# A tail of its own for the last full step, K norms from a triangle of the Gram matrix, and two attention answers moved

## What is computed

```python
xn = layernorm(x)
# attention, per batch, linear in the tokens
Q, K, V = xn @ Wq.T + bq, xn @ Wk.T + bk, xn @ Wv.T + bv
Q, K = Q / norm(Q, axis=tokens), K / norm(K, axis=tokens)
tailor = 1 / (256 + einsum('bnc,bc->bn', Q.T, K.sum(-1) + 1e-6))
s = xn + gamma * (V.sum(-1) + einsum('bnm,bmc->bcn', Q.T, einsum('bmn,bcn->bmc', K, V))) * tailor
# feed-forward, 704 hidden, activations and weights quantised to FP4 in blocks of 16
g = silu(fp4_linear(silu(fp4_linear(xn, w_gate)) * fp4_linear(xn, w_up), w_down))
out = x + s * g
```

## Time and profile before

| | |
|---|---|
| median of 3 runs | 596.38 us (595.67 to 596.96) |
| the profiled execution's own time | 597.39 us |
| its span in the trace | 595.3 us |
| busy: PE, DVE, ACT, POOL | 549.7, 555.4, 416.8, 265.6 us |
| mean granted TensorE clock | 0.991 |

### The profile page before, as it was taken

The page is one execution under the profiler, slowest core; times in us unless marked ns, Lnnn a source line. Parts: engine busy times, 40 slices in busy tenths (PEclk is TensorE's granted clock), DMA queues, the critical chain, the costliest instruction groups (busy, mean ns, idle before and its releaser), DMA issues. The chain is left out here.

```text
span 595.3 us, 15174 instructions
## 1 busy us (share of the span) xinstructions
PE 549.7 (92%) x4957; PEld 426.7 (72%) x4957; DVE 555.4 (93%) x1178; ACT 416.8 (70%) x901; POOL 265.6 (45%) x214
## 2 busy tenths in 40 slices
PE   0478999999999999999999989999999999999896
PEld 0355767777787777777887757778787777778775
DVE  7998999999999999999999998999999999977763
ACT  4979878877778777776777667877776776654421
POOL 7533333333433555355544453354743453423226
PEclk9999999999999999999999989999999999999999
DMA  8010000000011001111110111111011111132033
GB/s 251 18 37 19 19 20 19 19 20 19 19 37 37 19 3 55 55 55 55 55 55 2 54 58 55 56 55 54 2 55 55 55 37 37 36 103 95 0 124 143
DMA packets 17488, 29.14 MB, mean 49 GB/s; under 512 B 2688, under 2 KB 4864, under 8 KB 17408
## 3 DMA queue, kind: packets, MB, share of 16 engines
q1 hardware_dynamic: 17408, 28.13, 14.4%
HBM read 19.73 MB, written 8.39 MB: 47 GB/s over the span
## 5 line engine op out<-in xcount | busy, mean ns | idle before, releaser
L1427 PE MATMUL GU<-wgu,xqT 128*128 128x352 f16 x1536 | 252.8, 315 | 4.1 <-DVE h L953 2.6
L1427 PEld LDWEIGHTS GU<-wgu,xqT 128*128 128x128 f16 x1536 | 148.5, 99 | 78.3 <-issue 4.1
L546 POOL TENSOR_TENSOR ht<-h,hrr 128x1408 f32<-128x1408 f32 x32 | 82.9, 2590 | 80.5 <-DVE hrr L967 79.0
L635 ACT ACTIVATE sil<-GU,wkap 128x352 f32<-128x352 f32 x128 | 71.0, 555 | 60.0 <-PE GU L1427 59.1
L1437 PE MATMUL DS<-wdT,hqT 128*128 128x256 f16 x704 | 88.4, 275 | 1.9 <-ACT hqT L642 1.9
L953 DVE SCALAR_TENSOR_TENSOR h<-GU,wkap,sil 128x352 f32<-128x352 f32 x128 | 69.1, 540 | 11.9 <-ACT sil L635 8.0
L1001 DVE TENSOR_TENSOR hq<-hg,hs 128x704 f16<-128x704 f16 x128 | 79.1, 659 | 1.0
L1437 PEld LDWEIGHTS DS<-wdT,hqT 128*128 128x128 f16 x704 | 67.3, 99 | 12.5 <-ACT hqT L642 2.3
L505 POOL TENSOR_TENSOR xnat<-xs,xnat 128x510 f16<-128x510 f32 (+1 forms) x32 | 37.0, 1158 | 85.3 <-DVE hq L1001 72.9
L495 POOL TENSOR_TENSOR rs<-ve,half 128x2 f32<-128x2 f32 x32 | 22.9, 717 | 112.2 <-DVE ht L990 106.5
L671 ACT ACTIVATE gring<-DS,hun 128x256 f32<-128x256 f32 (+1 forms) x64 | 30.0, 468 | 44.9 <-issue 30.9
(11 more groups left out here) (166 smaller groups left out, 975.5 us busy)
## 6 DMA issues: line engine op xcount, KB each, us to landing
xin<-in_L_attn_x SPq DMA_DIRECT2D x34, 256.0 KB, 2.9
xe<-in_L_attn_x SPq DMA_DIRECT2D x25, 256.0 KB, 2.8
out<-o SPq DMA_DIRECT2D x25, 256.0 KB, 2.0
algebra<-in_L_ffn_w_down SPq DMA_DIRECT2D x1, 704.0 KB, 6.2
gring<-in_L_ffn_w_up SPq DMA_DIRECT2D x1, 640.0 KB, 4.8
xs<-in_L_attn_x SPq DMA_DIRECT2D x2, 256.0 KB, 4.2
xt<-in_L_attn_x SPq DMA_DIRECT2D x2, 256.0 KB, 4.7
out<-xin SPq DMA_DIRECT2D x2, 256.0 KB, 4.1
```

The source lines that it names most:

```text
L546: g.tensor_tensor(paired(ht[:, 0:2 * I]), paired(h[:, q]), spread(hrr[:, q], 4 * CB), ALU.mult).then_inc(S["ht_d"], 1)
L635: a.activation(sil[:, c], GU[:, c, 0, 0:CH], ACT.Silu, scale=wkap[:, 0:1]).then_inc(S["sil_d"], 1)
L1427: last = t.matmul(GU[:, c, m, 0:CH], xqT[:, k, j, 2 * a_ + kc], wgu[:, b_, kc, 2 * m + c], start=(z == 0 and kc == 0), stop=(z == 2 and kc ...
```

## The change

There are five edits. (1) K norms: G is symmetric, so t1k multiplies the diagonal blocks once and the lower block with a doubled copy of Wk, which ACT makes once (`wkT_twice`). (2) In the loop tables, gram1's answer moves in front of the mean and variance (`x_var`), and high_low's in front of the block maxima of x (`x_scales`, part 0). (3) p = 32 is taken out of `drive` for ACT, DVE and PE and written out by hand in their tails. (4) The last eight y's each get a place of their own, in h, ht, y and (for pair 31) the PSUM tile G; pair 24's x is loaded ahead too, into h, and POOL's add for pair 22 waits for the last scaled copy of pair 31. (5) The last pair's add is done by DVE, in halves, each stored by a DMA of its own.

```diff
-        ANSWERS = {(0, 0, 3): "gram0", (1, 0, 1): "gram1", ... (5, 0, 2): "high_low"}
+        ANSWERS = {(0, 0, 3): "gram0", (1, 0, 5): "gram1", ... (5, 0, 4): "high_low"}
@@ ACT, copy, at the start
+                    if i:
+                        a.activation(wkT_twice[:, :], G[:, D:2 * D], ACT.Copy, scale=2.0)
@@ PE, ask, t1k
                     for m in range(KD):
-                        for k in range(KD):
-                            last = t.matmul(G[:, m * D:(m + 1) * D], wkT[:, k, m * P:(m + 1) * P], Gs[:, k],
-                                            start=(k == 0), stop=(k == KD - 1))
+                        own = slice(m * P, (m + 1) * P)
+                        t.matmul(G[:, m * D:m * D + P], wkT[:, 0, own], Gs[:, 0, 0:P], start=True, stop=False)
+                        t.matmul(G[:, m * D:m * D + P], wkT_twice[:, own], Gs[:, 1, 0:P], start=False, stop=True)
+                        last = t.matmul(G[:, m * D + P:(m + 1) * D], wkT[:, 1, own], Gs[:, 1, P:D], start=True, stop=True)
@@ SP
+                        for j in range(2):
+                            own = slice(j * D, (j + 1) * D)
+                            sp.wait_ge(S["last_d"], j + 1)
+                            sp.dma_start(rows(of, e)[:, own], end_row(p)[:, own]).then_inc(S[f"out_d{ko}"], 16)
...
+                if isinstance(p, int) and p == PAIRS:
+                    sp.wait_ge(S["ht_d"], PAIRS - 1)
+                    sp.dma_start(h[:, 0, 0:2 * D], rows(xf, PAIRS - PB)).then_inc(S["x_mid_in"], 16)
@@ POOL, before the add
+                    if isinstance(e, int) and e == PAIRS - LAGE:
+                        pool.wait_ge(S["hloq"], 2 * PAIRS)
@@ DVE
+            def y_last(j):
+                return G[:, j * D:(j + 1) * D]
+            def o_last(j):
+                own = slice(j * D, (j + 1) * D)
+                dve.wait_ge(S["xend_in"], 16 * ENDS)
+                dve.wait_ge(S["y_d"], 4 * PAIRS - 2 + 2 * j)
+                v.tensor_tensor(xend[ENDS - 1][:, own], y_last(j), xend[ENDS - 1][:, own], ALU.add).then_inc(S["last_d"], 1)
...
             def tail():
+                p, k, b = PAIRS, PAIRS % 2, BATCHES - 1
+                e_half(p, k, 0, 0)
+                answer(b, "product")
+                parts(p, k, 0)
+                parts(p, k, 1)
+                e_half(p, k, 0, 1)
+                answer(b, "top")
+                answer(b, "high_low")
+                e_mul(p, k, 0)
+                e_mul(p, k, 1)
+                parts(p, k, 2)
+                h_round(p, k, 0)
+                e_mul(p + 1, 1 - k, 0)
+                h_round(p, k, 1)
+                e_mul(p + 1, 1 - k, 1)
+                h_round(p, k, 2)
+                e_mul(p + 2, k, 0)
+                e_mul(p + 2, k, 1)
+                h_round(p, k, 3)
+                for p in range(PAIRS + 3, PAIRS + LAGE):
                     for j in range(2):
                         e_mul(p, p % 2, j)
+                        if p == PAIRS + LAGE - 1:
+                            o_last(j)
@@ PE, tail
+                p, k = PAIRS, PAIRS % 2
+                s_half(p, k, 0, 0, last, PB - 5)
+                for c in range(2):
+                    hidden_transposes(p, k, 0, c, False)
+                ask(last, "product")
+                s_half(p, k, 0, 1, last, PB - 5)
+                down_product(p, k, 0)
+                ask(last, "top")
+                s_product(p, k, 0, last, False)
+                for c in range(2):
+                    hidden_transposes(p, k, 1, c, False)
+                ask(last, "high_low")
+                s_product(p, k, 1, last, False)
+                s_pair(PAIRS + 1 - LAGE)
+                down_product(p, k, 1)
-                p, k, first = PAIRS + 1, (PAIRS + 1) % 2, PAIRS + 1 - LAGE
+                p, k, first = PAIRS + 1, (PAIRS + 1) % 2, PAIRS + 2 - LAGE
                 s_pair(first)
                 s_pair(first + 1)
```

More of the change, by code:

```diff
@@ L213, in build @@
             nrm_d inv_d n_tr n_ev raw_mm raw_ev cs_mm cs_ev pm_mm den1 gi_d
[L214 removed]
+            tmp_d mt_d mtop_d last_d top_mm kap1 kap_d unm_d m_tr mhi_d mats""".split()
         S = {n: sem(n) for n in names}
@@ L264, in build @@
                 (5, 0, 1): "high_low"}
-        ANSWERS = {(0, 0, 3): "gram0", (1, 0, 1): "gram1", (1, 1, 0): "turn", (2, 1, 0): "squares",
-                   (3, 0, 0): "norms", (4, 0, 0): "tailor", (4, 0, 3): "scale", (4, 1, 0): "product", (4, 1, 2): "top", (5, 0, 2): "high_low"}
+        ANSWERS = {(0, 0, 3): "gram0", (1, 0, 5): "gram1", (1, 1, 0): "turn", (2, 1, 0): "squares",
+                   (3, 0, 0): "norms", (4, 0, 0): "tailor", (4, 0, 3): "scale", (4, 1, 0): "product", (4, 1, 2): "top", (5, 0, 4): "high_low"}
         COPIES = {(-4, 1, 0): "rows_1", (-3, 0, 1): "weights_v", (2, 0, 1): "t1q", (3, 1, 0): "raw"}
@@ L271, in build @@
                     (0, 1, 0): "gram1_0", (0, 1, 1): "gram1_1", (1, 0, 0): "turn", (1, 0, 2): "t1q",
-                    (1, 1, 1): "t1k", (2, 0, 0): "norms", (2, 0, 2): "raw", (2, 1, 1): "tailor", (3, 0, 0): "product",
-                    (3, 0, 1): "top", (3, 0, 3): "high_low"}
+                    (1, 1, 1): "t1k", (2, 0, 0): "norms", (2, 0, 2): "raw", (2, 1, 1): "tailor"}
         ANSWERS_END = {(0, 0, 2): "gram0", (0, 1, 2): "gram1", (1, 0, 1): "turn", (1, 1, 2): "squares",
-                       (2, 0, 1): "norms", (2, 1, 2): "tailor", (2, 1, 3): "scale", (3, 0, 0): "product",
-                       (3, 0, 1): "top", (3, 0, 4): "high_low"}
+                       (2, 0, 1): "norms", (2, 1, 2): "tailor", (2, 1, 3): "scale"}
         COPIES_END = {(1, 1, 0): "t1q", (2, 1, 0): "raw"}
@@ L303, in drive @@
                     iteration(b * PB + i, i % 2, b + later, step)
-            for p in range((BATCHES - 1) * PB + 4, PAIRS + 1):
+            for p in range((BATCHES - 1) * PB + 4, PAIRS if tail else PAIRS + 1):
                 iteration(p, p % 2, *batch_step(p))
@@ L324, in at_end, with y_place @@
         def at_end(p):
-            return isinstance(p, int) and p - LAGO >= PAIRS - ENDS
+            return isinstance(p, int) and p - LAGO >= PAIRS - PB
+        def y_place(e):
+            n = e - (PAIRS - PB) + 1
+            if n < 4:
+                return h[:, n // 2, n % 2 * 2 * D:(n % 2 + 1) * 2 * D]
+            return ht[:, (n - 4) * 2 * D:(n - 3) * 2 * D] if n < 7 else y[:, 0]
         def end_row(p):
-            return xend[p - LAGO - (PAIRS - ENDS)]
+            n = p - LAGO - (PAIRS - ENDS)
+            return h[:, 0, 0:2 * D] if n < 0 else xend[n]
         def s_beside(p, j, tail):
@@ L551, in iteration @@
                     g.tensor_tensor(inv[:, :], nrm[:, :], half[:, :], ALU.pow).then_inc(S["inv_d"], 1)
-                if on["o"]:
+                if on["o"] and not (isinstance(p, int) and p - LAGO == PAIRS - 1):
                     e, ko = p - LAGO, (k + LAGO) % 2
                     wait(pool, "y_d", 4 * e + 4)
+                    if isinstance(e, int) and e == PAIRS - LAGE:
+                        pool.wait_ge(S["hloq"], 2 * PAIRS)
+                    y_ = y_place(e) if isinstance(e, int) and e >= PAIRS - PB else y[:, ko]
                     if at_end(p):
-                        pool.wait_ge(S["xend_in"], 16 * ENDS)
-                        g.tensor_tensor(end_row(p), y[:, ko], end_row(p), ALU.add).then_inc(S["o_d"], 1)
+                        pool.wait_ge(*((S["x_mid_in"], 16) if e == PAIRS - PB else (S["xend_in"], 16 * ENDS)))
+                        g.tensor_tensor(end_row(p), y_, end_row(p), ALU.add).then_inc(S["o_d"], 1)
                     else:
@@ L1020, in e_mul @@
                 wait(dve, "g_d", n + 1)
-                if j == 0:
-                    wait(dve, "o_d", e - 1)
-                v.scalar_tensor_tensor(y[:, (k + LAGE) % 2, j * D:(j + 1) * D], GU[:, j, k, 0:D], unm[:, int(e >= PAIRS - PB):int(e >= PAIRS - PB) + 1],
+                if e < PAIRS - PB:
+                    if j == 0:
+                        wait(dve, "o_d", e - 1)
+                    to = y[:, e % 2, j * D:(j + 1) * D]
+                elif e == PAIRS - 1:
+                    to = y_last(j)
+                else:
+                    if j == 0 and e < PAIRS - 2:
+                        dve.wait_ge(S["ht_d"], PAIRS)
+                    if j == 0 and e == PAIRS - 2:
+                        dve.wait_ge(S["o_d"], PAIRS + 1 - LAGE)
+                    to = y_place(e)[:, j * D:(j + 1) * D]
+                v.scalar_tensor_tensor(to, GU[:, j, k, 0:D], unm[:, int(e >= PAIRS - PB):int(e >= PAIRS - PB) + 1],
                                        ring(gring, e, GRING)[:, j], ALU.mult, ALU.mult).then_inc(S["y_d"], 2)
@@ L1244, in iteration @@
                     x_front(p + 1, 1 - k)
+                attention(0, 5)
                 if on["xf"]:
```

18 lines of the change are left out of this document (12 added, 6 removed).

## The result

The changed kernel takes **592.77 us** (median of 5 runs, 592.69 to 593.2), the kernel before 596.38 on the same chip. The ratio is 0.9941 with a 95% interval of [0.9927, 0.9954]. The forecast was 591.1 in a range of 589.3 to 594.3, so sign and range hold, and 1.7 us of the expected gain of 5.3 are missing.

The account below looks back on a forecast made before the run. DVE was taken to set the pace up to p = 29, PE in p = 30 and 31, then DVE. -0.5 - 2.7 - 1.3 - 0.65 - 0.2 = -5.3 took 596.4 to 591.1 us, range 589.3 to 594.3.

Parts of the forecast that it names:

- Bounds of the loop: Loop: DVE sets the pace up to p = 29, so the moved answers bring 0 (bounds -1.5 to +1 us).
- Rival (c): Loop: PE bounds it after all, so t1k and PE's waits gain -3.9 us more, 587.2; chance 0.08.
- K norms: t1k: twelve narrow instructions take 1.32 us for 1.78, counting once, in the last batch: -0.5 us.
- Doubled copy: Start-up: ACT's copy of Wk takes 0.35 to 0.4 us, hidden by DVE: 0, or +0.4 if uncovered.
- p = 32 and pair 31's chain: p = 32: filling PE's hole avoids the clock fall and pair 31's first down product comes earlier: -2.7 us.
- Rival (a): After p = 32: PE's clock falls again at holes at 571 and 579 us, costing 1.6: 592.7; chance 0.18.
- (b): Pair 31's hidden chain is not earlier, rounding at 569.3 as before, so -2.7 goes: 593.7 us; chance 0.12.
- From the profile to the median: Whole kernel: differences worked out on one execution of 597.39 us were taken over to the median of 596.38.
- One pair less: End: eight instead of ten products of 0.655 us behind the last down product: -1.3 us.
- The last row: Last y to store issue: DVE's add in halves takes 1.2 us for 1.85 with POOL's add: -0.65 us.
- The halved store: Last store: half the bytes land sooner, -0.2 us (0 to 0.5 off; +0.3 if the end's three stores queue).
- The sum: Whole kernel: the gains add to -5.3 us, from 596.4 to 591.1 us.

Follow-up runs that it names:

- e_moves: The kernel before with only the moved answers of gram1 and high_low: 596.92 us, ratio 0.9996.
- The two small edits alone: Two runs of the kernel before, one with only the K norms edit (596.22 us), one with only the moved answers (596.92 us).
- e_hole: The changed kernel with PE at p = 32 asking top and high_low before the down product of pair 30's first half, as before: 594.25 us.
- e_nohold: The changed kernel without POOL's wait for pair 31's last scaled copy before its add for pair 22: 595.78 us.
- x_after: The changed kernel again, without an edit: 592.89 us, ratio 0.9931 to the kernel before.
- e_one: The changed kernel with the last row stored whole by one DMA after both of DVE's adds: 593.35 us.
- e_pool: The changed kernel with pair 31's add back on POOL and the pair stored whole by SP: 592.13 us.
- x_one: e_one again, in a later group of runs: 593.21 us, ratio 0.9934 to the kernel before.
- x_pool: e_pool again, in a later group of runs: 592.51 us, ratio 0.9924 to the kernel before.
- e_act: The changed kernel with pair 31 stored by one DMA from ACT's queue instead of two from SP's: 592.79 us.

## Why the prediction was nearly right, by its steps

**Bounds of the loop.** Right in kind. DVE's busy time and waits stayed, and PE's waits could go without a visible gain in e_moves. But the loop wasn't at zero: over the 28 pairs the profile has -0.79 (-0.43 and -0.36), where I put 0 with a bound of -1.5. The two small edits alone have -0.40 and -0.52 in the same stretches, each in one profile, and their medians do not settle it. The -0.43 is steady (180.39 to 180.43 in all eleven profiles of the changed order); the -0.36 is the most of them (273.97 to 274.28 for 274.33). PE's waits moved more than they went. Rival (c), -3.9, did not come.

**K norms.** Right, a little oversized. The twelve instructions take 1.40 us (536.74 to the next product at 538.14) for 1.78 where 1.32 was worked out, and -0.40 arrives on the path for the -0.46.

**Doubled copy.** Right: 0. It takes 0.47 us (said: 0.35 to 0.4) and DVE covers it.

**p = 32 and pair 31's chain.** Right in mechanism and nearly in size. The clock stayed at 1.00, the transposes took 0.61, the first rounding started at 567.76 (said: 567.7), the first down product at 575.41 (said: 575.6 less 0.5 for t1k). It is -2.47 for -2.7. e_hole shows that hole and order were the cause, and e_nohold that the wait on POOL guards this gain. Rival (a), a fall at the hole at 571 (0.91 us in PE's products), did not come in any profile of the changed order. My reason, that no hole is long, is weaker than it reads: in e_nohold PE idles for 1.59 us in the same place, longer than the 1.45 ahead of the fall, and keeps 1.00. (b) is excluded by 567.76.

**From the profile to the median.** This step had no reason given and is part of what is missing. All terms were worked out on one execution of 597.39 us in which the clock falls, and taken over to a median of 596.38. But 15 of 51 runs of this kernel have no fall (median 596.07), and there the 1.6 us of clock can't be won. Against the runs with less than 1.000 (597.24 in its group) x_after is 4.4 us faster, against those with 1.000 (596.05) 3.2 us. The -4.57 of the sum below belongs to the first kind; how many of the five runs behind 596.38 were of either kind isn't on record.

**One pair less.** -1.31 for -1.3.

**The last row.** Right in kind. e_one issues 0.68 us ahead of e_pool, but 0.16 of that lies ahead of the last product already; from the end of the products DVE's add puts the issue 0.53 us earlier, and x_one against x_pool says the same (said: 0.65). In the changed kernel itself 0.34 arrive by the end of the issue, as the two issues take 0.93 us for one of 0.33.

**The halved store.** This is the term that failed. It had -0.2, with a bound of +0.3 if the stores at the end queue. It came to +0.74. Halving by itself gave nothing (2.1 us for the undisturbed first half, 2.0 for a whole row), as the fixed part that I cited had warned. The same section of the Trainium skill has a part for the bytes too, which I left out. By it a half would land earlier, and no row shows that. The rest is not a queue of stores, which the bound had in mind, and not the half. The last bytes are under way when an instruction packet runs on the same DMA engines, and one of the sixteen reports comes late. Nothing in the prediction looked at what else the DMA engines carry at the end. The last two terms together were -0.85 and came to +0.40. With them undone the time is lower: x_pool is 0.7 us under x_one, and e_pool 0.7 under e_act, on the same chip each.

**The sum.** -0.40 - 0.79 - 2.47 - 1.31 - 0.34 + 0.74 = -4.57 by the table, and +0.76 of start-up that came late in that one profile gives the span's -3.8. The medians, where start-up evens out better, say -3.6 and -4.2; they mix runs with and without the fall. By the profile's table, against -5.3 the store lacks 0.9, the last row 0.3, pair 31 0.2 and t1k 0.1, and the loop brought 0.8 that had not been counted.

## What to carry to other kernels

At a kernel's end, count to the completion of the last store, and look in the DMA view at what else is under way then: here 0.53 us won ahead of an issue cost 1.2 behind it, with an instruction packet beside it in every such profile. A term read from one execution holds for executions like it; before carrying it to a median, look whether the others have the same clock. A hole of PE ahead of work on the path can cost twice, once itself and once by the lower clock after it; fill it with a product that is due anyway. And where DVE carries a chain of instructions with two SBUF inputs, hold POOL's work until the chain is through, if POOL has the slack.

## What the runs showed of the hardware that I had not expected

A last store of 256 KB lands 2.0 us after its issue, and after 3.2 (2.9 from another engine's queue) when an instruction packet of 8 KB runs beside its last bytes: one of its sixteen reports of completion comes late, and the DMA engines show nothing for the last 1.0 us (e_one). PE's granted clock fell to 0.50 at the second of two holes, of 1.45 and 0.45 to 0.50 us, in all four profiles that have them, yet 15 of 51 runs with the same code show a mean clock of 1.000. It did not fall behind a hole of 1.59 us in e_nohold:

```profile
571.60:573.00 1.40, 0.00 (x0) 0.00 (x0) 1.40 (x3) 0.00 (x0) 0.00 (x0) 1.00 0.49 187
```

At the loop's back edge every version has PE without work for 2.1 to 2.6 us and DVE for 2.5 to 2.8 us; the clock fell there in five of the fourteen profiles (before, e_moves, e_hole, e_pool, x_one) and stayed in the other nine. A POOL add of half the columns takes 0.71 us for 1.26, so 0.16 us of it do not shrink.
